# Row statistics with two homes, and 32x32 block turns by VectorE in place of TensorE's turns, in a four-layer cross-attention kernel

## The chip, the cores and the metric

The kernel runs on one core of one Trainium2 chip. The metric is the device time of one execution in microseconds (us). The core's engines run side by side, each through its own list of instructions in order, and they meet only at semaphores: TensorE (PE in the profile, PEld for its weight loads), VectorE (DVE), ScalarE (ACT), GpSimd (POOL) and SyncE (SP, which here only starts DMA transfers). Operands lie in SBUF, products of TensorE in PSUM, which has eight banks of 128 partitions by 512 numbers. All arithmetic is float32.

## What is computed

The input x and the context have 16 batches of 128 rows by 256 columns. Four layers follow each other:

```
x = L0(x, ctx)   # self attention, cross attention (16 heads of 16), then a mixture of 8 experts, 2 per row
x = L1(x, ctx)   # ten chosen rows of each batch attend to ctx and are replaced
x = L2(x, ctx, mask)
x = L3(x, ctx)   # cross attention with normed queries and a residual
```

The change is in the attention programs of L0 and L3, and in L2, which is grouped-query attention and a gated feed-forward:

```python
h, kv = rmsnorm(x, ln1), rmsnorm(ctx, ln1)
q = rope(h @ Wq)            # 16 heads of 64
k, v = rope(kv @ Wk), kv @ Wv   # 4 heads of 64, each shared by 4 query heads
p = softmax(q @ k.T / 8 + mask)  # per head 128 x 128
x = x + (p @ v) @ Wo
n = rmsnorm(x, ln2)
x = x + (silu(n @ Wgate) * (n @ Wup)) @ Wdown   # 1024 wide
```

## The kernel before

A batch has 128 rows, one to a partition. The program is a row of stages: one call of `attention` does L0's self attention and cross attention (32 batches one after the other), then routing and experts, then L1 for groups of four batches, then L2, then a second call of `attention` for L3. The whole order is written by hand: in each stage every engine has a loop over slots t, and in slot t it does parts that belong to batches t-3 to t+3.

**The attention programs (L348 on).** Slot t has the scores of batch t+1 (`scores`, L491), their maxima on VectorE (L831, two reductions of 128x1024 numbers), the maxima turned by TensorE (L630) and subtracted from the queries (L867), the scores again with keys on the partitions (`scores_turned`, L501), the exponentials on ScalarE (L737), and the products with the values (`products`, L512) of batch t-1. Normalization works in groups of GB = 4 batches. VectorE takes the statistics of batch t+11 at the end of slot t (`row_stats`, L808 to L815) into the tiles `st` and `mv`. GpSimd takes a group's `mv` when all four are there, writes the normed rows `xn_a` and, where the context is normed too (cross attention of L0), `cn_a`, with four instructions each at L769, and adds the output bias (L776). `st` and `mv` have one home for x and one for the context, each with room for one group. So `row_stats` of the first batch of group g waits until GpSimd is through with group g-1 (`hx_ok`, and `hc_ok` for the context).

**L2 (slots t = 0 to 16).** TensorE does in slot t, in this order: scores of batch t (`scores`, L2061, 32 matrix products that contract over 32 rows, four row tiles of the array at a time, into banks 0 to 3, one bank for each key head); the output projection of batch t-1 (`rows_out`, L2089); queries of t+1 (L1407 in two banks); the first of four turns of the probabilities (`turn`, L2071); keys and values of t+1 (L1420, L1423); the second turn; the turn of the middle rows of t-1 (`turn_mid`, L2096) and of the input rows of t+2 (L1432); the third turn; the gate projection `g0`, the fourth turn, `u0`, `g1`, `u1` (all L1407); the products of batch t (L2081); and the down projection of t-1 (L2089). A turn is four 128x128 transposes into bank 4, and ScalarE copies the bank to `turned_probs` (`turned_copy`, L2161). `products` makes one product of 64x512 for each key head, two of them at a time in two column halves of the array, into banks 5 and 6.

Between scores and turn a head group i goes VectorE `mask_max` (L2298, L2301), ScalarE `exps` (L2152, four instructions), VectorE `divide` (L2306), GpSimd `scale` (L2227). The middle chain of batch t-1 goes `out_copy` (L2182) on ScalarE, `rows_out` "wo", VectorE `add_rows` and `stats_mid` (L2277 to L2284), GpSimd `rms_mid` (L2221), VectorE `scale_mid` (L2290), `turn_mid`, ScalarE `mid_copy` (L2168), the gate and up projections, ScalarE `silu` (L2175), VectorE `gate` (L2312), the down projection. The table `SLOT_JOBS` says which bank each job has. `job_claim` makes TensorE wait until the bank's job before has been read out (`job_moved`).

## Time and profile before

| | us |
|---|---|
| median of 3 runs | 1411.53 |
| the runs | 1411.53, 1416.6, 1411.37 |
| the profiled execution | 1418.67 |
| its span, first to last instruction | 1416.9 |

The page of the profile gives for each engine its busy time over the span. It cannot say what an engine is worth in a stage, so the stages are read one by one: in the timelines, which list each engine's instructions with their start and with the idle time ahead of them and who ended it, and in the view of stretches, which gives the busy time of each engine and the granted clock of TensorE between two times. The attention call for L0 has its slots from about 36 to 280 us, the experts end about 700 us, L2 runs from 810 to 1246 us and L3 from 1256 us to the end.

### The profile page before, as it was taken

The page shows a single profiled execution, that of the slowest core. Times are in us where ns is not written, and L with a number is a line of the kernel's source. Part 1 is how long each engine was busy: PE and PEld are TensorE (multiplying, and loading weights), DVE is VectorE, ACT ScalarE, POOL GpSimd, SP SyncE. Part 2 cuts the span into 40 slices and gives each one's busy share as a digit, 9 for nine tenths or more (in the row PEclk, how much of TensorE's full clock was granted, in tenths as well). Part 3 has the DMA queues.
Part 4 walks back from the last instruction along what each step waited for, and adds up shares of the span by engine and source line. Part 5 has one row for each costly group of instructions (what it writes and reads, how often), then busy time and mean ns, then how long its engine had stood idle before and what let it go on. Part 6 is the DMA issues. An engine that isn't in the chain of part 4 may idle for free. (4 is left out here: it accounts for less than half of the span.)

```text
span 1416.9 us, 32778 instructions
## 1 busy us (share of the span) xinstructions
PE 1264.0 (89%) x13114; PEld 1044.7 (74%) x13114; DVE 681.5 (48%) x1613; ACT 644.4 (45%) x1496; POOL 430.3 (30%) x545
## 2 busy tenths in 40 slices
PE   4898899886799999999588799999999999858986
PEld 2566666665589999999477678888888888735665
DVE  3686777767422000000564564544544544237775
ACT  2454555422444445544212165655655655325542
POOL 3224446243323222235100152432432432123200
PEclk9999999966799999999656899999999999989997
DMA  9000000000389999997410000000000000000000
GB/s 300 2 2 2 2 2 17 9 17 23 109 299 336 330 357 355 350 341 260 156 32 2 3 1 2 1 2 1 1 1 1 2 1 2 0 0 2 17 16 31
DMA packets 80038, 120.02 MB, mean 85 GB/s; under 512 B 12112, under 2 KB 62544, under 8 KB 79760
## 3 DMA queue, kind: packets, MB, share of 16 engines
q1 hardware_dynamic: 73840, 106.62, 22.4%
q0 software_dynamic: 4768, 10.26, 2.0%
q8 instruction: 105, 1.72, 0.5%
q10 hardware_dynamic: 1280, 1.04, 0.2%
q14 instruction: 45, 0.37, 0.1%
HBM read 108.43 MB, written 9.48 MB: 83 GB/s over the span
## 5 line engine op out<-in xcount | busy, mean ns | idle before, releaser
L1590 ACT ACTIVATE w_ca<-scores,fc1b 128x128 f32<-128x128 f32 x312 | 114.2, 368 | 139.8 <-PE scores L1545 118.7
L1545 PEld LDWEIGHTS scores<-reg 128*128 128x128 f32 x1248 | 145.1, 192 | 7.8 <-DMA reg<-in_fc 2.8
L1545 PE MATMUL scores<-reg 128*128 128x128 f32 x1248 | 146.4, 275 | 4.3 <-DMA reg<-in_fc 1.8
L1555 PE MATMUL bank<-reg,w_ca 128*128 128x256 f32 x624 | 141.1, 379 | 0.3 <-DVE small L1615 0.3
L2152 ACT ACTIVATE reg<-reg,mx 128x128 f32<-128x128 f32 x256 | 99.2, 389 | 88.0 <-DVE mx L2301 87.7
L831 DVE TENSOR_REDUCE reg<-scores 128x8 f32<-128x1024 f32 x96 | 112.9, 1219 | 49.6 <-PE scores L491 49.4
L1624 DVE TENSOR_TENSOR reg<-bank,reg 128x256 f32<-128x256 f32 x39 | 16.6, 425 | 241.6 <-PE bank L1555 233.3
L2227 POOL TENSOR_TENSOR reg<-reg,rden 128x512 f32<-128x512 f32 x64 | 66.7, 1042 | 212.1 <-DVE rden L2306 212.0
L1555 PEld LDWEIGHTS bank<-reg,w_ca 128*128 128x128 f32 x624 | 115.6, 190 | 14.5 <-DVE small L1615 0.3
L1407 PE MATMUL scores<-reg 128*128 128x128 f32 x1024 | 122.0, 278 | 0.5 <-ACT reg L2168 0.5
L1407 PEld LDWEIGHTS scores<-reg 128*128 128x128 f32 x1024 | 119.3, 195 | 0.7 <-ACT reg L2168 0.7
L2089 PE MATMUL bank<-reg,w_ca 128*128 128x256 f32 x512 | 118.8, 385 | 0.8 <-issue 0.8
L2089 PEld LDWEIGHTS bank<-reg,w_ca 128*128 128x128 f32 x512 | 94.7, 190 | 26.6 <-issue 13.2
L737 ACT ACTIVATE reg<-scores 128x1024 f32<-128x1024 f32 x96 | 92.9, 1021 | 39.2 <-PE scores L501 35.7
L671 ACT ACTIVATE reg<-bank,qk_bias,shape_c 128x512 f32<-128x512 f32 x96 | 69.7, 780 | 55.5 <-PE bank L474 55.2
L501 PE MATMUL scores<-reg 32*128 32x128 f32 x1536 | 64.3, 308 | 32.6 <-DVE reg L831 31.6
L501 PEld LDWEIGHTS scores<-reg 32*128 32x128 f32 x1536 | 54.9, 208 | 48.8 <-issue 48.7
L970 POOL DMA_INDIRECT expert_out<-reg,block_ids_of x39 | 38.7, 992 | 143.7 <-DMA expert_out<-reg,block_ids_of 79.5
L2312 DVE TENSOR_TENSOR w_ca<-scores,w_ca 128x512 f32<-128x512 f32 x32 | 22.1, 692 | 109.1 <-PE scores L1407 109.1
L491 PEld LDWEIGHTS scores<-reg 32*128 32x128 f32 x1536 | 50.0, 192 | 29.8 <-ACT reg L737 21.4
L732 ACT ACTIVATE reg<-bank,shape_c 128x256 f32<-128x256 f32 x48 | 22.8, 474 | 104.3 <-DVE reg L341 104.3
L491 PE MATMUL scores<-reg 32*128 32x128 f32 x1536 | 59.7, 290 | 8.8 <-ACT reg L737 6.6
(277 smaller groups left out, 2383.7 us busy)
## 6 DMA issues: line engine op xcount, KB each, us to landing
reg<-in_fc SPq DMA_DIRECT2D x78, 1024.0 KB
reg<-expert_out SPq DMA_DIRECT2D x16, 256.0 KB, 3.7
xres<-in_x SPq DMA_DIRECT2D x4, 512.0 KB, 10.7
ctxr<-in_ctx SPq DMA_DIRECT2D x1, 2048.0 KB, 14.8
w_l<-in_w_l SPq DMA_DIRECT2D x2, 1024.0 KB, 12.1
routed_rows<-reg SPq DMA_DIRECT2D x8, 256.0 KB
out<-xres SPq DMA_DIRECT2D x8, 256.0 KB, 2.1
w_sa<-in_w_sa SPq DMA_DIRECT2D x1, 1024.0 KB, 8.6
```

Of the source, the lines that this page charges most:

```text
L491: ins = nc.tensor.matmul(S[r][:, (2 * s + c) * P:(2 * s + c + 1) * P], Qs[rows_of(r), (b // GB) % 2, s, c, batch(b)], Ks[rows_of(r), (b // ...
L501: ins = nc.tensor.matmul(S[r][:, (2 * s + c) * P:(2 * s + c + 1) * P], Ks[rows_of(r), (b // GB) % 2, s, c, batch(b)], Qs[rows_of(r), (b // ...
L671: ins = nc.scalar.activation(dst[:, g % 2, s, m, :], bank[:, :], ACT.Identity, scale=scale[:, s:s + 1], bias=bias[:, s, m:m + 1])
L737: ins = nc.scalar.activation(PT2[:, t % 2, 2 * half:2 * half + 2, :, :, :].rearrange("p r s c q -> p (r s c q)"), scores4[:, 2 * half:2 * ...
L831: ins = nc.vector.tensor_reduce(mxpad.rearrange("p (c n d) -> p n c d", c=C, d=DH)[:, 4 * half:4 * half + 4, :, 0], scores4[:, 2 * half:2 ...
L1407: ins = nc.tensor.matmul(bank[:, k * P:(k + 1) * P], w[:, c, w0:w0 + P], src[:, c, :], start=(c == 0), stop=(c == C - 1))
L1545: ins = nc.tensor.matmul(S[n % 4][:, 0:P], up_w8[j % 2][:, c, f * P:(f + 1) * P], xbT[:, j % 2, c, :], start=(c == 0), stop=(c == C - 1))
L1555: ins = nc.tensor.matmul(T[j % 2][:, 0:D], h1[:, j % 2, f, :], down_w8[j % 2][:, f, :], start=(f == 0), stop=(f == FC - 1))
L1590: nc.scalar.activation(h1[:, j % 2, f, :], S[n % 4][:, 0:P], ACT.Gelu, bias=fc1b[:, bass.ds(e * FC + f, 1)]).then_inc(M["fc1_free"], 1)
L2089: ins = nc.tensor.matmul(bank[:, 0:D], src[:, f, :], w[:, f, :], start=(f == 0), stop=(f == FC - 1))
L2152: ins = nc.scalar.activation(v[:, a, :], v[:, a, :], ACT.Exp, bias=cols_of(mx, n)[:, a:a + 1], accum_out=cols_of(psum, n)[:, a:a + 1])
L2227: nc.gpsimd.tensor_tensor(v, v, spread(rden, n), ALU.mult).then_inc(M["l2_scaled"], 1)
```

## The change

It has two parts.

**Two homes for row statistics.** `st` and `mv` get four places in place of two: a pair (x, context) for even groups and one for odd groups. `row_stats` of group g now waits for GpSimd's group g-2, and only from g = 2 on.

**L2's probabilities are turned by VectorE.** The transposes of TensorE and ScalarE's copies go. `turn` is now one VectorE instruction for each head group, SBUF to SBUF, which transposes each 32x32 block within its place: a row strip of 32 partitions then holds, for the 32 query rows of that strip, 32 keys on the partitions in each of four blocks k. So `products` contracts over 32 rows at a time: for each strip r of four, key block k of four and key head of four one product of 64x128, 64 in all, accumulated over k. Strip r has a bank of its own (0 to 3), two key heads use its column halves. Each strip needs all values at its own 32 partitions. SyncE therefore writes the values of each batch to DRAM (`values_dram`, 128 KB) and reads them back four times (4 x 128 KB) into `values4`, which lies in `w_sa`. `out_copy` is four copies of 128x256 in place of two of 128x512. The order of the slot and `SLOT_JOBS` change with it: `turn_in` and `turn_mid` come ahead of keys and values, the transposed middle rows and the down projection use bank 4, and GpSimd does `rms_mid` ahead of all four `scale`s.

The core of the diff:

```diff
-        st = sb("st", [P, 2, GB, 6])
-        mv = sb("mv", [P, 2, GB, 2])
+        st = sb("st", [P, 4, GB, 6])
+        mv = sb("mv", [P, 4, GB, 2])
...
-                        if g > 0 and j == 0:
-                            dve.wait_ge(M["hx_ok"], GB * g)
-                            if norms == 2 and stage_of(g - 1)["kv"] == "norm":
-                                dve.wait_ge(M["hc_ok"], GB * (g % G))
+                        if g > 1 and j == 0:
+                            dve.wait_ge(M["hx_ok"], GB * (g - 1))
+                            if norms == 2 and stage_of(g - 2)["kv"] == "norm":
+                                dve.wait_ge(M["hc_ok"], GB * (g % G - 1))
+                        k = 2 * (g % 2)
...
-        SLOT_JOBS = [("wo", -1, "a"), ("qa", 1, "b"), ("qb", 1, "c"), ("kv", 1, "a"), ("xt", -1, 0), ("at", 2, 1),
-                     ("g0", -1, 2), ("u0", -1, 3), ("g1", -1, 0), ("u1", -1, 1), ("pv0", 0, "a"), ("pv1", 0, "b"), ("d", -1, "c")]
+        SLOT_JOBS = [("wo", -1, "a"), ("qa", 1, "b"), ("qb", 1, "c"), ("at", 2, 0), ("xt", -1, "t"), ("kv", 1, "a"),
+                     ("g0", -1, 1), ("u0", -1, 2), ("g1", -1, 3), ("u1", -1, 0),
+                     ("pv0", 0, 0), ("pv1", 0, 1), ("pv2", 0, 2), ("pv3", 0, 3), ("d", -1, "t")]
...
+                for b in range(B):
+                    sp.wait_ge(M["l2_values_ok"], b + 1)
+                    if b >= 2:
+                        await_done(sp, "pv3", b - 2)
+                    own_rows = values_dram[b * P:(b + 1) * P, :]
+                    sp.dma_start(own_rows, values2[:, b % 2, :, :].rearrange("p h d -> p (h d)")).then_inc(values_out, 16)
+                    sp.wait_ge(values_out, 16 * (b + 1))
+                    for r in range(4):
+                        sp.dma_start(values4[32 * r:32 * r + 32, b % 2, :, :], own_rows.rearrange("(k p) n -> p k n", p=32))\
+                            .then_inc(values_in[b % 2], 16)
...
                 def products(b):
                     pe.wait_ge(M["l2_pt_ok"], 4 * b + 4)
-                    pe.wait_ge(M["l2_values_ok"], b + 1)
+                    pe.wait_ge(values_in[b % 2], 16 * 4 * (b // 2 + 1))
+                    out_banks = [job_claim(pe, f"pv{r}", b) for r in range(4)]
                     for q in range(2):
-                        bank = job_claim(pe, f"pv{q}", b)
-                        for half in range(2):
-                            i = 2 * q + half
-                            ins = nc.tensor.matmul(bank[half * HD:(half + 1) * HD, :], values2[:, b % 2, i, :],
-                                                   turned_probs[:, b % 2, A4 * i:A4 * (i + 1), :].rearrange("p a q -> p (a q)"),
-                                                   start=True, stop=True)
-                        ins.then_inc(job_done(f"pv{q}", b), 1)
+                        for k in range(4):
+                            for half in range(2):
+                                i = 2 * q + half
+                                for r in range(4):
+                                    own = slice(32 * r, 32 * r + 32)
+                                    ins = nc.tensor.matmul(out_banks[r][half * HD:(half + 1) * HD, q * P:(q + 1) * P],
+                                                           values4[own, b % 2, k, i * HD:(i + 1) * HD],
+                                                           turned_probs[own, b % 2, A4 * i:A4 * (i + 1), 32 * k:32 * k + 32],
+                                                           start=(k == 0), stop=(k == 3))
+                                    if q == 1 and k == 3 and half == 1:
+                                        ins.then_inc(job_done(f"pv{r}", b), 1)
...
+                def turn(b, i):
+                    n = 4 * b + i
+                    dve.wait_ge(M["l2_scaled"], n + 1)
+                    if b >= 2:
+                        await_done(dve, "pv3", b - 2)
+                    nc.vector.transpose(turned_tile(n).rearrange("p a k -> p (a k)"), bank_of(n)[0].rearrange("p a k -> p (a k)"))\
+                        .then_inc(M["l2_pt_ok"], 1)
```

TensorE, one steady slot of L2, before. The first row is `scores`; L2071 is a turn:

```order
L2061 MATMUL scores<-reg 128x128 x32
L2089 MATMUL bank<-reg,w_ca 128x256 x8
L1407 MATMUL bank<-reg 128x128 x16
L2071 MATMUL bank<-ident,reg 128x128 x4
L1420 MATMUL bank<-reg 128x128 x4
L1423 MATMUL bank<-reg 128x256 x2
L2071 MATMUL bank<-ident,reg 128x128 x4
L2096 MATMUL scores<-ident,reg 128x128 x2
L1432 MATMUL scores<-ident,reg 128x128 x4
L2071 MATMUL bank<-ident,reg 128x128 x4
L1407 MATMUL scores<-reg 128x128 x8
L2071 MATMUL bank<-ident,reg 128x128 x4
```

The rows go on with a turn, 24 of L1407 (`u0`, `g1`, `u1`), L2081 and L2089. The same slot in the changed kernel, L2076 being `scores`, L2100 a projection of rows, L1412 queries and then gate and up, L2090 the products:

```order
L2076 MATMUL scores<-reg 128x128 x32
L2100 MATMUL bank<-reg,w_ca 128x256 x8
L1412 MATMUL bank<-reg 128x128 x16
L1437 MATMUL scores<-ident,reg 128x128 x4
L2107 MATMUL bank<-ident,reg 128x128 x2
L1425 MATMUL bank<-reg 128x128 x4
L1428 MATMUL bank<-reg 128x256 x2
L1412 MATMUL scores<-reg 128x128 x32
L2090 MATMUL scores<-reg,w_sa 64x128 x64
L2100 MATMUL bank<-reg,w_ca 128x256 x8
L2076 MATMUL scores<-reg 128x128 x32
```

The four turns are gone from between the projections, the products stand in the same place with 64 instructions in place of 4 and write the banks named `scores`, and the next slot's scores follow after the down projection.

VectorE in a slot of L2, before, from the fourth maximum to the second multiply (L2306 `divide`, L1475 and L1476 `rope` of the queries, L2290 `scale_mid`, L2312 `gate`):

```order
L2301 TENSOR_REDUCE mx<-reg 128x4
L2306 RECIPROCAL rden<-psum 128x4
```

In the changed kernel (L2285 the fourth maximum, L2290 `divide`, L2297 the new turn, L2304 `gate`, L1461 the statistics of the inputs):

```order

```

The four turns stand between the rope products and the statistics of batch t+3. The second multiply, L2304 again, comes after these statistics, as before.

## Rows read from the trace of the kernel before

**Rows 1.** the page, part 1: busy us of TensorE, share of the span, instructions.

```profile
PE 1264.0 (89%) x13114; PEld 1044.7 (74%) x13114; DVE 681.5 (48%) x1613; ACT 644.4 (45%) x1496; POOL 430.3 (30%) x545
```

**Rows 2.** timeline of TensorE, one steady slot: start us, us, line, form, count, idle before.

```profile
854.13 2.07 PE L2061 MATMUL scores<-reg 32*128 32x128 f32 x64
856.13 3.72 PE L2089 MATMUL bank<-reg,w_ca 128*128 128x256 f32 x16
859.69 3.73 PE L1407 MATMUL bank<-reg 128*128 128x128 f32 x32
863.26 0.60 PE L2071 MATMUL bank<-ident,reg 128*128 128x128 f32 x4
863.69 1.06 PE L1420 MATMUL bank<-reg 128*128 128x128 f32 x8
...
866.92 0.63 PE L2071 MATMUL bank<-ident,reg 128*128 128x128 f32 x4 [0.21 <-ACT reg L2161]
...
869.61 5.52 PE L1407 MATMUL scores<-reg 128*128 128x128 f32 x48
875.06 1.94 PE L2081 MATMUL bank<-reg 128*64 128x512 f32 x8
876.93 3.72 PE L2089 MATMUL bank<-reg,w_ca 128*128 128x256 f32 x16
880.58 1.62 PE L2061 MATMUL scores<-reg 32*128 32x128 f32 x48
```

**Rows 3.** timeline of VectorE, same slot: the second multiply of the gated feed-forward.

```profile
875.17 0.69 DVE L2312 TENSOR_TENSOR w_ca<-scores,w_ca 128x512 f32<-128x512 f32 x1 [1.94 <-PE scores L1407]
```

**Rows 4.** timeline of TensorE, stage of chosen tokens: two forms in small tiles.

```profile
784.40 1.90 PE L1719 MATMUL scores<-reg,w_ca 32*32 32x128 f32 x128
...
794.12 3.77 PE L1737 MATMUL scores<-w_ca,reg 32*128 32x32 f32 x128
```

**Rows 5.** groups by line and form, whole span: busy us, mean ns; idle before.

```profile
L2152 ACT ACTIVATE reg<-reg,mx 128x128 f32<-128x128 f32 x256 | 99.2, 389 | 88.0 <-DVE mx L2301 87.7
...
L2227 POOL TENSOR_TENSOR reg<-reg,rden 128x512 f32<-128x512 f32 x64 | 66.7, 1042 | 212.1 <-DVE rden L2306 212.0
...
L2298 DVE SCALAR_TENSOR_TENSOR reg<-scores,reg 128x512 f32<-128x512 f32 x64 | 43.5, 679 | 19.7 <-PE scores L2061 19.7
...
L341 DVE STREAM_TRANSPOSE reg<-bank 128x512 f32<-128x512 f32 x48 | 34.1, 711 | 11.2 <-PE bank L512 9.6 <-remote 1.4
...
L2168 ACT ACTIVATE reg<-scores 128x256 f32<-128x256 f32 x16 | 6.1, 380 | 10.0 <-PE scores L2096 10.0
```

**Rows 6.** timeline of TensorE, the last slot that has products.

```profile
1218.89 1.94 PE L2081 MATMUL bank<-reg 128*64 128x512 f32 x8
```

**Rows 7.** the page, part 6: DMA issues: count, KB each, us to landing.

```profile
reg<-expert_out SPq DMA_DIRECT2D x16, 256.0 KB, 3.7
```

**Rows 8.** timeline of three engines around one stop, first attention program.

```profile
119.23 4.85 POOL L769 TENSOR_SCALAR reg<-ctxr,mv,rstd 128x256 f32<-128x256 f32 x4
...
124.17 0.43 DVE L808 BATCH_NORM_STATS2 st<-xres 128x6 f32<-128x256 f32 x1 [6.66 <-issue]
...
127.59 2.09 PE L501 MATMUL scores<-reg 32*128 32x128 f32 x32 [4.25 <-DVE reg L831]
```

**Rows 9.** the line of the row statistics: what ended its idle time, us, times.

```profile
  issue: 18.1, 3
```

**Rows 10.** busy us of engines by stretch: PE, PEld, DVE, ACT, POOL; then clock granted.

```profile
80.51:97.05 16.54, 16.48 (x229) 11.59 (x230) 13.44 (x27) 8.86 (x13) 8.46 (x9) 1.00 0.01 2
111.29:134.84 23.55, 19.30 (x229) 13.65 (x230) 13.29 (x28) 8.96 (x13) 15.06 (x16) 0.86 0.01 2
149.01:170.14 21.13, 18.46 (x233) 12.30 (x234) 13.32 (x28) 10.64 (x16) 15.11 (x16) 1.00 0.01 2
184.31:206.73 22.42, 20.07 (x233) 13.47 (x234) 13.99 (x31) 10.75 (x16) 15.07 (x16) 0.92 0.01 2
1287.61:1306.05 18.44, 16.70 (x225) 10.86 (x226) 12.64 (x23) 10.57 (x15) 7.76 (x8) 1.00 0.01 2
```

119 lines of the change are left out of this document (48 added, 71 removed).

## Prediction, made before the changed kernel was run

> **What bounds the kernel now.** I read the page first: TensorE is busy for 89% of the span [rows 1], so a change pays where it shortens TensorE's list or a wait of TensorE. Both parts sit in stages that repeat, so I went on to timelines of one slot each. In L2 the steady slot is 26.45 us long, from one `scores` to the next (854.13 to 880.58), and TensorE is without work in it for 0.21 us only, ahead of the third turn [rows 2]. VectorE meanwhile stands idle for 1.94 us even ahead of the slot's last multiply [rows 3]. So L2 is bound by TensorE's list, and work moved to VectorE is free until a chain gets late. In the attention programs the heavy slots are TensorE's too, but in the cross attention of L0 there are three stops in which VectorE waits at the row statistics, 18.1 us in all [rows 9]. The profile calls them "issue". The rows of the first one say what it is: GpSimd's four normalizations of the context start at 119.23 and take 4.85 us, and VectorE goes on at 124.17, after 6.66 us; TensorE then stood still for 4.25 us until 127.59 [rows 8].
>
> **Part 1, two homes for statistics.** The stop is a wait of group g's first statistics for GpSimd's group g-1. What is queued behind it on VectorE are the maxima of the next batch, which TensorE needs for the turned scores. With two homes the wait is for group g-2, which GpSimd ended four slots earlier, so the stop goes. What is late next is TensorE itself, which used part of the stop to work ahead; the gain is therefore not 18.1 us. I compare pairs of slots with and without a stop [rows 10]. [...] That is 7.0 us. Cross attention without one, from the last program: 18.44 us; with one 21.13 and 22.42, so 2.7 and 4.0 us. Sum 13.7 us. The last program has two such waits before its slots get going; there TensorE is not ready earlier, and I count nothing. Bounds: 8.1 us, if each stop gives back only the second one's 2.7, with no help of the clock, and 18.1 us, VectorE's whole idle time [rows 9].
>
> **Part 2, L2, a steady slot.**
> - Removed from TensorE: four turns. One takes 0.43 us of its list (863.26 to 863.69), four 1.72, and the wait of 0.21 goes with them: -1.93 us [rows 2].
> - Products: before 1.87 us (875.06 to 876.93) [rows 2]. Now 64 products, each two records as all float32 products here, so 128 records of 128 columns in tiles of 32x64, eight of them in the array. No row shows this form. With four tiles (`scores`) 64 records take 2.00 us (854.13 to 856.13) [rows 2], 31 ns each, 125 ns for each tile. With sixteen tiles of 32x32 and also 128 columns, 128 records take 1.90 us, 14.8 ns each [rows 4]. Eight tiles at 125 ns each would give 15.6 ns, above the 14.8 that the chip keeps up: 2.0 us. I take 2.0 us, +0.13. Ends: 1.9 us by sixteen tiles, 4.0 us if only four tiles run at a time.
> - A new wait. The products' four banks are 0 to 3, and bank 0 holds `u1` until VectorE's second multiply has read it. Before, that multiply ran beside the products: it starts at 875.17 and takes 0.69 [rows 3], and the products start at 875.06 [rows 2]. Now they can start at 875.86: +0.80 us. Behind the wait on TensorE stand the products and the down projection, nothing that another engine could cover.
> - The next slot's scores need the same four banks, so four copies of 128x256 on ScalarE, at most 0.38 each [rows 5] or 1.5 us. They run beside the down projection, 3.65 us [rows 2]: nothing.
> - VectorE gets four turns. The nearest row is the 32x32 turn of 128x512 out of PSUM, 0.71 us; the multiply of the same size takes 0.68 [rows 5]. 2.8 us in a slot in which VectorE has idle time to spare. Their place decides. From the slot's start: scores end at 2.0; maximum pairs take twice 0.68 us; the third pair now waits for the output projection (856.13 to 859.69, so 5.6) and the middle statistics and ends at 8.2; then the exponentials of group 2 (four of 0.39) at 9.8, those of group 3, after two copies, at 12.3; GpSimd's fourth scale (1.04) at 14.4 [rows 5]. VectorE, in its order, reaches turn 3 at about 16.1 after the first multiply and ends at 16.8. TensorE ends `u1` at 26.45 less turns and wait (1.93), products (1.87) and down projection (3.65), which is 19.0. So the turns have over 2 us of cover; a slot 2 us faster would lay them bare.
> - The middle chain: `turn_mid` now stands at about 9.6 on TensorE; the scaled middle rows are ready at about 8.7, ScalarE's copy at 10.7; gate and up projections take 4/3 of the 5.45 us that three of their four parts show (869.61 to 875.06) [rows 2], 7.3, so they start at 19.0 - 7.3 = 11.7. Covered by 1 us. GpSimd's `rms_mid` ahead of the scales puts these back by 1.4 us, within the 2 us above.
> - Values through DRAM: a write and four reads of 128 KB. A read of 256 KB lands in 3.7 us [rows 7], so some 8 us, with over 30 us between the values' copy and the products. SyncE has nothing else queued in L2. Nothing.
>
> So -1.93 + 0.13 + 0.80 = -1.00 us in a slot, and there are 14 such slots (t = 1 to 14): -14.0.
>
> **The slots at the ends.** t = 15 has no queries and keys. Slot starts lie 26.45 us apart, so it starts at 880.58 + 12 x 26.45 = 1198.0, and its products at 1218.89 [rows 6], 20.9 in. There turns and gate projection wait for each other. Now the gate projections can start with the middle copy at 10.6 and end at 17.9, the products start at 18.7: -2.2, with their own +0.13 it is -2.1. t = 0 has no down projection: the next scores wait openly for the last copies, some 1.3 us, the chain of turns behind rope products on VectorE costs about 0.5 and the products 0.13: +1.9. L2 together: -14.0 - 2.1 + 1.9 = -14.2 us.
>
> **Sum.** 13.7 + 14.2 = 27.9 us. Against the profiled execution, 1418.67, this gives 1390.8. That execution is 7.1 us over the median of the runs; the same saving from the median 1411.53 gives 1383.6; I forecast 1383.5.
>
> [...] The row of the sixteen tiles has a record every 14.8 ns [rows 4]. [...]
>
> **The rivals.**
> 1. *The width of the weights counts.* With weights 128 wide and only 32 columns to stream, 128 records take 3.77 us, 29.5 ns each; with weights 32 wide 14.8 [rows 4]. A straight line between gives 19.7 ns for 64, or 2.5 us. 16 slots by 0.5 us: 1391.5. Against it: with 125 ns for a tile, a load half as wide as in `scores` should hide.
> 2. *A charge for each record binds.* Halfway between the same two rows lie 22 ns, 2.8 us: 16 slots by 0.8: 1396.5. Against it: the 14.8 ns are themselves a bound on any such charge. [...]
> 3. *Four tiles at a time.* If column halves of a row strip exclude each other, 4.0 us: +2.0 in 16 slots, 32 us, against 27.9 saved: 1415.5. Against it: the old products already ran two column halves at once (their 128*64 form), and the sixteen tiles beat this rate by two.
> 4. *Slower: load and stream of a row strip follow each other.* A record of 128 columns takes 3.57 us / 32 = 112 ns (859.69 to 863.26) on the whole array [rows 2], a load of 64 columns half of 4 x 29.5, so 59 ns. Together 171 ns, over four strips 43 ns a record and 5.5 us: +3.5 in 16 slots is 56 us, 1439.5. Slower begins where the products pass 3.8 us, 29 ns a record. Against it: sixteen tiles of 32x32 spend 4 x 14.8 = 59 ns a record and strip, less than the 112 of the stream alone. [...]
> 5. *Part 1 gives less.* Each stop gives 2.7 us, 8.1 in all, and the clock does not change: 1389.
>
> **Chances.** Forecast 0.58, rival 5 0.08, rival 1 0.12, rival 2 0.10, rival 3 0.07, rival 4 0.05. The range 1375 to 1406 leaves out rivals 3 and 4 and a little on both sides: the forecast with all 18.1 us of part 1 and products of 1.9 us is 1377.5, rival 2 with 8.1 us of part 1 is 1402, and about 3 us either way are the spread of the runs (1411.37 to 1416.6). About 0.5%, 7 us, is what a measurement of this kernel can tell from no change. Below 1404.5: 0.82; within 7 us of 1411.5: 0.11; above: 0.07.
>
> **What would show it.** Right: the L2 slot at about 25.45 us; the products' 128 records in 2.0 us; 0.8 us idle ahead of them, ended by the second multiply; no idle time of VectorE at the row statistics from 110 to 200 us, the pairs of slots at 16.5 and 18.4. Wrong: products above 2.5 us, TensorE waiting for the new VectorE turn, or for the middle copy ahead of the gate projection; a half clock where TensorE was warm.

## The result and the profile after

The changed kernel takes 1392.85 us (median of 4 runs, 1389.38 to 1398.77), the kernel before 1412.88 us in the runs beside it (4 runs, 1411.37 to 1416.6): ratio 0.9859, 95% interval 0.9819 to 0.9899, or 20.0 us less. The forecast was 1383.5 in a range of 1375 to 1406. The time is inside the range and on the side that was forecast, 9.3 us above the point; most of what follows is about these 9 us. The profiled execution of the changed kernel took 1392.40 us, span 1390.6; that of before 1418.67, span 1416.9.

The page, part 1 (busy us of each engine, share of the span, instructions), to be read beside [rows 1]. TensorE lost 34 us of work and is busy for 88% of the span; VectorE's busy time grew by 48 us, and its turns alone take 43.6:

```profile
PE 1230.0 (88%) x14778; PEld 1035.2 (74%) x14778; DVE 729.9 (52%) x1677; ACT 611.3 (44%) x1464; POOL 428.7 (31%) x545
```

The groups by line, new or changed (busy us, mean ns of one, then the idle time ahead of them and what ended it):

```profile
L2297 DVE STREAM_TRANSPOSE reg<-reg 128x512 f32<-128x512 f32 x64 | 43.6, 689 | 0.0
...
L2090 PE MATMUL scores<-reg,w_sa 32*64 32x128 f32 x2048 | 35.0, 282 | 19.2 <-issue 14.2 <-DVE reg L2297 5.1
...
L2176 ACT ACTIVATE w_ca<-scores 128x256 f32<-128x256 f32 x64 | 19.4, 390 | 69.5 <-PE scores L2090 69.5
...
L2274 DVE TENSOR_SCALAR reg<-xres,small 128x256 f32<-128x256 f32 x16 | 17.2, 1073 | 2.2 <-POOL small L2208 1.5
```

A turn on VectorE takes 689 ns (forecast from rows of 0.68 and 0.71 us) and VectorE never waited ahead of one. One copy of the products takes 390 ns (380). The products' idle time of 14.2 us is put down to "issue", and 5.1 to the turns, which is the first slot alone. The last row is a surprise: VectorE's scale of the middle rows took 1073 ns on average, where the same instruction took 0.34 us in most slots before.

**A steady slot of L2.** TensorE's timeline (start us, us, line, form, count, idle time before), the slot that answers to [rows 2]:

```profile
862.95 2.07 PE L2076 MATMUL scores<-reg 32*128 32x128 f32 x64
864.94 3.72 PE L2100 MATMUL bank<-reg,w_ca 128*128 128x256 f32 x16
868.50 3.73 PE L1412 MATMUL bank<-reg 128*128 128x128 f32 x32
872.07 0.60 PE L1437 MATMUL scores<-ident,reg 128*128 128x128 f32 x4
872.51 0.40 PE L2107 MATMUL bank<-ident,reg 128*128 128x128 f32 x2
...
874.50 7.31 PE L1412 MATMUL scores<-reg 128*128 128x128 f32 x64
882.75 2.09 PE L2090 MATMUL scores<-reg,w_sa 32*64 32x128 f32 x128 [0.94 <-issue]
884.76 3.96 PE L2100 MATMUL bank<-reg,w_ca 128*128 128x256 f32 x16
888.65 0.61 PE L2076 MATMUL scores<-reg 32*128 32x128 f32 x12
```

From 862.95 to 888.65 it is 25.70 us; this one has a down projection of 3.96 us, most have 3.72 and last 25.46 to 25.48. The mean of the fourteen is 25.50 us, where before had 26.45. The 128 records of the products (L2090; a record is one row of the trace, and each of the 64 products leaves two) run from 882.75 to the next start at 884.76: 2.01 us, 15.7 ns each. They start after 0.94 us without work. VectorE in the same slot:

```profile
871.29 1.12 DVE L2274 TENSOR_SCALAR reg<-xres,small 128x256 f32<-128x256 f32 x1
...
876.10 0.70 DVE L2297 STREAM_TRANSPOSE reg<-reg 128x512 f32<-128x512 f32 x1
...
876.78 0.68 DVE L2297 STREAM_TRANSPOSE reg<-reg 128x512 f32<-128x512 f32 x1
...
878.02 0.69 DVE L2297 STREAM_TRANSPOSE reg<-reg 128x512 f32<-128x512 f32 x1
878.64 0.65 DVE L2304 TENSOR_TENSOR w_ca<-scores,w_ca 128x512 f32<-128x512 f32 x1
879.21 0.69 DVE L2297 STREAM_TRANSPOSE reg<-reg 128x512 f32<-128x512 f32 x1
...
881.85 0.69 DVE L2304 TENSOR_TENSOR w_ca<-scores,w_ca 128x512 f32<-128x512 f32 x1 [1.02 <-PE scores L1412]
```

From the fourth maximum on VectorE's order is: the rope products of the queries, the first two turns with a reciprocal between them, the rope products of the keys, the third turn, the first multiply of the feed-forward, the fourth turn, the statistics of batch t+3, the second multiply. The four turns end at 879.9, 2.9 us ahead of the products. The slot's second multiply (L2304, the last row) starts when `u1` is done, and ends at 882.54; the products start 0.2 us behind that. So the wait stands where the forecast put it, although the profile names it "issue".

**Part 1.** The stops at the row statistics (L811, L808 before) are gone: no "issue" as in [rows 9] is left in the line's idle time, which lists 5.3 us for the first load of x and 10.3 us for TensorE at the start of L3. Windows over pairs of slots, from score to score (busy us of PE, PEld, DVE, ACT, POOL with their counts, then the granted clock), answering to [rows 10]:

```profile
110.73:127.27 16.54, 16.49 (x229) 11.60 (x229) 14.40 (x32) 9.19 (x13) 14.90 (x16) 1.00 0.01 3
141.43:159.88 18.45, 18.40 (x232) 12.28 (x233) 15.04 (x32) 11.15 (x16) 15.29 (x16) 1.00 0.01 2
174.04:192.49 18.45, 18.40 (x232) 12.28 (x233) 15.45 (x30) 11.15 (x16) 15.11 (x16) 1.00 0.01 1
```

16.54 us in self attention and 18.45 in cross attention, which are the 16.54 and 18.44 of the pairs without a stop; all at the full clock (1.00).

**The slots at the ends.** The first slot (t = 0) and the last with products (t = 15):

```profile
791.29 3.79 PE L2076 MATMUL scores<-reg 32*128 32x128 f32 x64 [1.78 <-DVE xres L2023]
...
806.92 3.65 PE L2090 MATMUL scores<-reg,w_sa 32*64 32x128 f32 x128 [5.07 <-DVE reg L2297]
812.00 2.07 PE L2076 MATMUL scores<-reg 32*128 32x128 f32 x64 [1.43 <-ACT w_ca L2176]
```

```profile
1169.03 2.07 PE L2076 MATMUL scores<-reg 32*128 32x128 f32 x64
...
1178.55 0.44 PE L2107 MATMUL bank<-ident,reg 128*128 128x128 f32 x2 [3.81 <-DVE reg L2274]
1179.46 8.81 PE L1412 MATMUL scores<-reg 128*128 128x128 f32 x64 [0.47 <-ACT reg L2162]
1189.21 2.09 PE L2090 MATMUL scores<-reg,w_sa 32*64 32x128 f32 x128 [0.94 <-issue]
```

The first slot takes 20.71 us, and took 17.65 before (810.04 to 827.69 in that trace). The last one takes 20.18 from its scores to its products; before it was 20.95. Its gate and up projections took 8.81 us, since the granted clock was 0.50 of full speed from 1179.0 to 1182.4; 7.31 us is what they take in the steady slot above, at 1.00.

**Where the 26.3 us between the two spans went.** Up to the first product of the routing: 262.76 before, 249.57 after, -13.2. From there to the first scores of L2, where the change touches nothing: 547.3 and 541.7, -5.6. First slot +3.1, fourteen steady slots -13.2, t = 15 to the start of L3 -0.6, L3 +3.2.

### The profile page after: what moved, and what is told of

It reads as the page before. It is cut to its first block and busy times, and to the rows that moved or that the text cites. A ratio compares the mean times of both kernels' runs of the same rounds, so it can differ in the third digit from the quotient of the medians.

```text
span 1390.6 us, 36276 instructions
## 1 busy us (share of the span) xinstructions
PE 1230.0 (88%) x14778; PEld 1035.2 (74%) x14778; DVE 729.9 (52%) x1677; ACT 611.3 (44%) x1464; POOL 428.7 (31%) x545
## 3 DMA queue, kind: packets, MB, share of 16 engines
q8 instruction: 118, 1.93, 0.6%
q10 hardware_dynamic: 1280, 1.04, 0.2%
## 5 line engine op out<-in xcount | busy, mean ns | idle before, releaser
L1560 PEld LDWEIGHTS bank<-reg,w_ca 128*128 128x128 f32 x624 | 115.6, 190 | 14.4 <-DVE small L1620 0.3
L1412 PEld LDWEIGHTS scores<-reg 128*128 128x128 f32 x1024 | 119.7, 196 | 2.1 <-ACT reg L2162 1.4
L1412 PE MATMUL scores<-reg 128*128 128x128 f32 x1024 | 120.2, 279 | 0.9 <-ACT reg L2162 0.9
L2100 PE MATMUL bank<-reg,w_ca 128*128 128x256 f32 x512 | 119.0, 386 | 0.9 <-issue 0.8
L2100 PEld LDWEIGHTS bank<-reg,w_ca 128*128 128x128 f32 x512 | 94.7, 190 | 17.4 <-issue 4.0
L503 PE MATMUL scores<-reg 32*128 32x128 f32 x1536 | 60.7, 297 | 23.3 <-DVE reg L834 23.3
L503 PEld LDWEIGHTS scores<-reg 32*128 32x128 f32 x1536 | 51.5, 199 | 38.8 <-issue 38.7
L2261 DVE TENSOR_TENSOR xres<-bank,xres 128x256 f32<-128x256 f32 x32 | 13.6, 424 | 110.4 <-PE bank L2100 110.4
L493 PEld LDWEIGHTS scores<-reg 32*128 32x128 f32 x1536 | 49.8, 194 | 28.3 <-ACT reg L739 21.3
L2205 POOL TENSOR_TENSOR small<-small 128x1 f32<-128x1 f32 x16 | 3.1, 193 | 205.0 <-DVE small L2268 205.0
L493 PE MATMUL scores<-reg 32*128 32x128 f32 x1536 | 59.0, 292 | 7.9 <-ACT reg L739 7.3
```

What stands on the lines that cost most here:

```text
L493: ins = nc.tensor.matmul(S[r][:, (2 * s + c) * P:(2 * s + c + 1) * P], Qs[rows_of(r), (b // GB) % 2, s, c, batch(b)], Ks[rows_of(r), (b // ...
L503: ins = nc.tensor.matmul(S[r][:, (2 * s + c) * P:(2 * s + c + 1) * P], Ks[rows_of(r), (b // GB) % 2, s, c, batch(b)], Qs[rows_of(r), (b // ...
L1412: ins = nc.tensor.matmul(bank[:, k * P:(k + 1) * P], w[:, c, w0:w0 + P], src[:, c, :], start=(c == 0), stop=(c == C - 1))
L1560: ins = nc.tensor.matmul(T[j % 2][:, 0:D], h1[:, j % 2, f, :], down_w8[j % 2][:, f, :], start=(f == 0), stop=(f == FC - 1))
L2100: ins = nc.tensor.matmul(bank[:, 0:D], src[:, f, :], w[:, f, :], start=(f == 0), stop=(f == FC - 1))
```

## Experiments

All are of the same kernel family; ratios are to the kernel before in the runs beside them, which gave 1413.87 us (17 runs) for the first four, 1418.28 (7 runs) for the next four and 1420.33 (8 runs) for the last three. The kernels of the last two groups are therefore compared by their ratios and by their traces.

**1 and 2. Each part alone.** First the kernel before with the two homes and nothing else:

```diff
-        st = sb("st", [P, 2, GB, 6])
+        st = sb("st", [P, 4, GB, 6])
...
-                        if g > 0 and j == 0:
-                            dve.wait_ge(M["hx_ok"], GB * g)
+                        if g > 1 and j == 0:
+                            dve.wait_ge(M["hx_ok"], GB * (g - 1))
...
```

> The kernel before with part 1 alone: st and mv have two homes, row_stats waits for GpSimd's group g-2. My theory: the three stops of VectorE in the cross attention of L0 go (7.0 + 2.7 + 4.0 us by pairs of slots), so 13.7 us less than before, and the start of L3 stays as it is. Rival A, part 1 is worth its stops and nothing else but moves TensorE's clock windows at the start of L3 for the worse, as the changed kernel's trace shows there (slots of 8.5, 10.0 and 10.1 us in place of 6.9, 9.2 and 9.3): then 10 to 11 us less and the same long slots in this kernel's L3. Rival B, the fall of the clock there is chance: the L3 slots are short here.

Measured: 1401.27 us (6 runs), ratio 0.9914, interval 0.9897 to 0.9931, or 12.6 us less. The first product of the routing stands at 249.04, 13.7 us before that of the kernel before. That this is the term of part 1 to the tenth is partly luck, since the point varies by more than 1 us between executions: it stands at 261.40 and not at 262.76 in the next kernel, which has one home too, and at 248.2 to 250.1 in the other traces with two. At least a part of that comes from the clock long before the stops: the granted clock was 0.50 for 3.4 us from about 55 us on in the traces of the kernel before, the changed one and this one, and 1.00 there in those of experiments 2 and 3. Traces that are alike in this give 13.2 and 13.7 us for part 1, and 12.4 (261.40 against 248.98).

L3 took 161.7 us here from its first product to the end, against 157.9 in the kernel before, as rival A expects. But in the traces of experiments 4 and 6, which have two homes too, it took 157.4 and 157.9, and in that of experiment 2, with one home, 161.1. So the homes don't decide it; rival B, chance, is what is left.

Then the changed kernel with the same lines put back, that is, the turns on VectorE alone:

> The changed kernel with part 1 undone: one home for the statistics, all of L2 as changed. My theory: the stops in L0 are back (13 to 14 us over the changed kernel), L2's slot is 25.5 us and its products take 2.0 us as in the changed kernel. From scores of batch 0 to the first product of L3 the changed kernel needs 10.8 us less than the kernel before; so this one should be 10 to 11 us faster than before. Rival: with part 1 gone the L3 start is fast again, then 13 to 14 us.

Measured: 1405.76 us (6 runs), ratio 0.994, interval 0.9919 to 0.996, or 8.1 us less; expected were 10 to 11. In its trace L2 takes 10.1 us less than before from its first scores to the start of L3, and L3 3.2 us more. The two parts add up to 20.7 us, and the change as a whole measured 20.0: no sign that they work on each other. The whole is short of 27.9 mainly by the second part (8.1 against 14.2), less by the first (12.6 against 13.7). In this kernel, too, nothing is changed from the routing to L2, and the stretch took 543.6 us; in the kernel with the homes alone it took 540.8. In the kernels of experiments 5, 6, 7 and 11, which have the same work there as the changed one, it took 546.7 to 547.2. So it varies by several us between executions, and the -5.6 above are not shown to be the change's.

**3. The wait for bank 0.** The second up-projection goes to a bank that is free at that time:

```diff
-                      ("g0", -1, 1), ("u0", -1, 2), ("g1", -1, 3), ("u1", -1, 0),
+                      ("g0", -1, 1), ("u0", -1, 2), ("g1", -1, 3), ("u1", -1, "b"),
```

> The changed kernel with one entry of SLOT_JOBS changed: u1 goes to bank 6 (home b, free since the rope of the queries) in place of bank 0. My theory: the wait of 0.94 us ahead of the products is that for u1's bank, so it goes, VectorE's second multiply runs beside the products again, and nothing else is near: slot 25.50 - 0.94 = 24.56 us, 14 slots and t = 15, 14 us less than the changed kernel. Rival: another wait stands right behind it (the fourth VectorE turn, or the values from DRAM), then 0 to 5 us and the profile names it.

Measured: 1377.14 us (5 runs, 1375.05 to 1380.37), ratio 0.9744, interval 0.9726 to 0.9762: 15.7 us faster than the changed kernel, and faster than both. TensorE's timeline has no idle time at the products:

```profile
879.12 1.95 PE L1412 MATMUL bank<-reg 128*128 128x128 f32 x16
881.00 2.10 PE L2090 MATMUL scores<-reg,w_sa 32*64 32x128 f32 x128
```

Slots are 24.48 us apart, 1.02 less than in the changed kernel. That shows what the 0.94 us of "issue" were: the wait for the reader of bank 0, with its semaphore.

**4. How many tiles run at a time.** The changed kernel with the column half as the outermost loop of the products, so that four tiles are in use at a time and not eight:

```diff
-                    for q in range(2):
-                        for k in range(4):
-                            for half in range(2):
+                    for half in range(2):
+                        for q in range(2):
+                            for k in range(4):
```

> The changed kernel with the loops of products in another order: all of column half 0 first, then all of half 1, so that only the four row strips of one half can run at the same time; same 64 products. Theory 1, a tile gives one record of 128 columns in 125 ns and the number of tiles at work decides: 128 records at 31 ns, 4.0 us in place of 2.0, +2.0 in 16 slots, 32 us slower than the changed kernel. Theory 2, a charge of some 15 to 16 ns for each record decides and tiles don't: still 2.0 us, no change.

Measured: 1409.64 us (10 runs), ratio 0.9978, interval 0.996 to 0.9996: 16.8 us slower than the changed kernel, halfway between the two theories. The products:

```profile
889.92 3.36 PE L2090 MATMUL scores<-reg,w_sa 32*64 32x128 f32 x128 [0.94 <-issue]
893.22 3.72 PE L2100 MATMUL bank<-reg,w_ca 128*128 128x256 f32 x16
```

128 records in 3.30 us are 25.8 ns each, 103 ns for each of four tiles. Tiles count, so the forecast's account stands only in part: eight tiles are needed for 2.0 us, but a tile of 32x64 comes free after 103 ns and not after the 125 of `scores` with its 128 columns of weights. By 103 ns eight tiles would give 12.9 ns a record; what they do give is 15.7. So something other than the tiles sets the products' pace in the changed kernel.

**5. The fourth turn ahead of the input statistics.** This part of the change undone:

```diff
-                    if now:
-                        turn(t, 3)
                     if is_batch(t + 3):
                         l2_stats_in(dve, link, t + 3)
+                    if now:
+                        turn(t, 3)
```

> The change with its smallest part undone: the fourth turn stands behind the input statistics on VectorE again. In the trace of the change the fourth turn ends 16.9 us into a slot, the statistics behind it take 1.2 us (four instructions, 0.38 + 0.41 + 0.18 + 0.15), and the products start at 19.8. Theory 1: the move is worth nothing, since the turn would end at 18.1 and still be 1.7 us early: the slots stay at 25.50 us and the total at 1393 us, within 2. Rival: the products' idle time of 0.94 us is in truth a wait for the fourth turn (the profile infers releasers): then the slots grow by up to 1.2 us, to 26.7, and the total by up to 19 us, to 1412.

Measured: 1400.52 us (4 runs), ratio 0.9863, interval 0.9825 to 0.99; the change has 0.9859. Most slots are 25.46 to 25.50 us apart, with the same 0.94 us ahead of the products. This move is worth nothing, and the wait isn't one for the turn.

**6. The length of the cover.** In the kernel of experiment 3 the fourth turn goes behind the second multiply, to the very end of VectorE's slot:

```diff
-                    if now:
-                        turn(t, 3)
...
                     if before_now:
                         gate(t - 1, 1)
+                    if now:
+                        turn(t, 3)
```

> The change with the second up-projection in a bank of its own (1377.1 us), and with the fourth turn as VectorE's last work of a slot, behind the second gating multiply. In that kernel's trace this multiply ends at 881.80, 0.80 us after the products start (881.00), so the fourth turn would end at 882.5. Theory 1: the wait is now in sight and costs what the times say: the products start 1.5 us later, and with some 0.15 us for the semaphore a slot takes 24.48 + 1.6 = 26.1 us; over 16 slots some 25 us, 1402. It tells how long the cover of the turns is: 1.9 us in that kernel, from the turn's end at 879.1 to the products at 881.0. Rival: the products' start isn't set by the turns even then (TensorE would be late for another reason): 1377.

Measured: 1401.12 us (4 runs), ratio 0.9883, interval 0.985 to 0.9916, against 0.9744. The products now wait for the turn:

```profile
862.04 2.09 PE L2090 MATMUL scores<-reg,w_sa 32*64 32x128 f32 x128 [1.40 <-DVE reg L2297]
```

The slots grow from 24.48 to 25.95 us, by 1.47 (expected 1.6). So the cover of the turns (the time for which a late turn costs nothing) ends where the times say, and the releaser that the profile names is here the right one.

**7. The scale that takes three times as long.** In the kernel of experiment 3 GpSimd's first multiply waits until VectorE has scaled the middle rows:

```diff
                         for i in range(4):
+                            if i == 0 and is_batch(t - 1):
+                                pool.wait_ge(M["l2_mid_ok"], t)
                             scale(t, i)
```

> The change with the second up-projection in a bank of its own, and GpSimd's first scaling of a slot waits until VectorE has scaled the middle rows. Theory 1: the middle scale took 1.12 us in place of 0.35 because GpSimd's 1.04 us multiply ran beside it; now it takes 0.35 us again, at the same start (8.3 us into the slot), and GpSimd's scaling starts 0.4 us later, which its cover hides. The steady slot stays at 24.48 us; in the last slot (t=15), where TensorE waits for the middle rows, 0.8 us are won. Total 1376.3, not to be told from 1377.1 by the time alone; the row of the scale decides. Rival: the longer scale comes from something else (its place behind the reciprocal, its operand): it stays at 1.1 us.

Measured: 1378.86 us (4 runs), ratio 0.9712, interval 0.9682 to 0.9742. In the changed kernel VectorE's scale starts at 871.29 (above), and GpSimd's timeline has, for its first two multiplies:

```profile
871.22 2.08 POOL L2214 TENSOR_TENSOR reg<-reg,rden 128x512 f32<-128x512 f32 x2
```

With the wait VectorE's scale reads:

```profile
873.85 0.35 DVE L2276 TENSOR_SCALAR reg<-xres,small 128x256 f32<-128x256 f32 x1
```

and GpSimd's multiplies behind it:

```profile
874.28 2.04 POOL L2214 TENSOR_TENSOR reg<-reg,rden 128x512 f32<-128x512 f32 x2 [0.47 <-DVE reg L2276]
```

1.12 us beside GpSimd's multiply, 0.35 without it. In the kernel before the scale took 0.34 us, because GpSimd's order was another: its third multiply started at 863.58 and took 1.04, and VectorE's scale came as that ended:

```profile
864.60 0.34 DVE L2290 TENSOR_SCALAR reg<-xres,small 128x256 f32<-128x256 f32 x1
```

That trace confirms the cause by itself. In its slot t = 15 GpSimd's third multiply started at 1207.38, just ahead of the scale, and the scale was the only long one of its 16:

```profile
1207.41 1.16 DVE L2290 TENSOR_SCALAR reg<-xres,small 128x256 f32<-128x256 f32 x1
```

In both traces the scale ends with the multiply that it met: in the changed kernel it started 0.07 us after a multiply of 1.04 us (871.22) and ended 0.15 us after that multiply, and in the kernel before, at t = 15, it started 0.03 us after one of 1.04 us and ended 0.15 us after it. The 32x32 turns kept their 0.7 us beside the same multiplies: the second, at 876.78, took 0.68 with GpSimd's fourth multiply from 876.94 on. Why the scale is held up and the turn is not, no row shows. In the slot t = 15 TensorE waits 3.04 us for the middle rows, where it was 3.81, and the 0.77 us are what the scale lost. They don't reach the end: there three of the four projections behind it took 8.07 us in place of the 7.47 of experiment 3, at a mean granted clock of 0.68 in place of 0.74, and from scores to products the slot took 20.0 against 19.9. In the steady slots, too, the long scale is covered: they are 24.45 us apart with the wait and 24.48 without. The total can't tell the two kernels apart.

**8. Column halves that follow each other.** In the kernel of experiment 3, eight tiles as before, but the two halves of a row strip directly one behind the other:

```diff
-                            for half in range(2):
-                                i = 2 * q + half
-                                for r in range(4):
-                                    own = slice(32 * r, 32 * r + 32)
+                            for r in range(4):
+                                own = slice(32 * r, 32 * r + 32)
+                                for half in range(2):
+                                    i = 2 * q + half
```

> The change with the second up-projection in a bank of its own, and in the products the two column halves of one row strip follow each other (the four row strips outside), in place of four row strips of one column half and then four of the other. Eight tiles are in use in both. Theory 1: what counts is how many records pass before a tile comes again (8 in both), so 128 records take 2.0 us as before and the total stays at 1377. Rival: two records in a row on one row strip hold each other up, as two loads of weights into the same rows would: then a pair costs up to what a row strip's record costs in the scores (31 ns), 64 pairs 2.0 to 4.0 us, up to 2.0 us more in each of 16 slots, up to 1409.

Measured: 1380.34 us (4 runs), ratio 0.9742, interval 0.9706 to 0.9778, as experiment 3. 128 records again take 2.02 us, in slots of 24.48. This order within the eight tiles made no difference, and a row strip took two records in a row at no price: rivals 3 and 4 of the prediction don't hold even there.

**9 and 10. What sets 15.7 ns.** In the kernel of experiment 3 each record is split into two of 64 columns; the products are the same, the weights are loaded twice as often:

```diff
-                        for k in range(4):
+                        for c, k in [(c, k) for c in range(2) for k in range(4)]:
                             for half in range(2):
...
-                                    ins = nc.tensor.matmul(out_banks[r][half * HD:(half + 1) * HD, q * P:(q + 1) * P],
+                                    ins = nc.tensor.matmul(out_banks[r][half * HD:(half + 1) * HD, at:at + 64],
...
-                                                           turned_probs[own, b % 2, A4 * i:A4 * (i + 1), 32 * k:32 * k + 32],
+                                                           turned_probs[own, b % 2, a0:a0 + 2, 32 * k:32 * k + 32],
```

> The change with the second up-projection in a bank of its own (slot 24.48 us, 1377.1 us), with each instruction of the products split into two of 64 columns: 256 records in place of 128 for the same products, eight tiles in turn as before, the same weights loaded twice. Theory 1: with eight tiles a record costs a charge of its own of about 15.7 ns, whatever its columns: the products take 4.0 us in place of 2.0, a slot 26.5 us, the total 1377 + 16 x 2.0 = 1409. Rival: the columns that stream through the tiles set the time (103 ns for 128 columns in one tile, shared by eight, is 12.9 ns): 64 columns cost half, the products stay at 2.0 to 2.1 us and the total at 1377.

And the same with the column half outermost, four tiles at a time:

> The kernel with the split columns, and the column half as the outermost loop, so that only four tiles are in use at a time: 256 records of 64 columns. With 128 records of 128 columns over four tiles a record took 25.8 ns, 103 ns for a tile. Theory 1: most of a tile's 103 ns is the load of its weights and the streaming of 128 columns, one behind the other; with 64 columns the tile takes 103 less the time of 64 columns, by their pace at full clock in the keys' products of this kernel (32 records of 128 columns in 1.95 to 3.73 us, 58 to 61 ns each on a single tile) some 29 ns: 74 ns a tile, 18.5 ns a record, 4.7 us for 256 records, so a slot of 27.2 us. Rival: the tile is kept by its columns alone (0.8 ns a column): 51 ns a tile, 12.9 ns a record, which the charge of a record lifts to 15.7: 4.0 us, as with eight tiles, and a slot of 26.5 us.

Measured: 1432.66 us (5 runs), ratio 1.0084, interval 1.0052 to 1.0116, and one run of 1430.92. TensorE at the products, eight tiles first:

```profile
892.11 1.65 PE L2091 MATMUL scores<-reg,w_sa 32*64 32x64 f32 x134
895.07 1.54 PE L2091 MATMUL scores<-reg,w_sa 32*64 32x64 f32 x122 [1.32 <-issue]
...
947.43 2.46 PE L2091 MATMUL scores<-reg,w_sa 32*64 32x64 f32 x207
951.82 0.78 PE L2091 MATMUL scores<-reg,w_sa 32*64 32x64 f32 x49 [1.93 <-issue]
```

and four tiles:

```profile
892.48 2.10 PE L2091 MATMUL scores<-reg,w_sa 32*64 32x64 f32 x134
...
948.29 3.15 PE L2091 MATMUL scores<-reg,w_sa 32*64 32x64 f32 x207
```

134 records take 1.65 us and 207 take 2.46, so 0.81 / 73 = 11.1 ns for each with eight tiles, and (3.15 - 2.10) / 73 = 14.4 ns with four. In four tiles, then, a record holds its tile for 58 ns with 64 columns and for 103 with 128: there the columns count, 0.7 ns each (an estimate from these two figures), beside some 12 ns of something else. In eight tiles half the columns bring 15.7 down to 11.1 ns only, though the tiles would allow 58 / 8 = 7.2. So neither theory holds as written: a record isn't charged 15.7 ns whatever its columns, and the tiles' own time isn't what limits eight of them. What does stays open. The 74 ns for a tile in the expectation of the four tiles rest on a row read wrongly: 1.95 us is the time of 16 such records and 3.73 that of 32, so one takes 112 to 122 ns and not 58 to 61.

The whole time is worse still, for a reason that none of them expected: TensorE stands idle once inside the products of every slot but the first, for 1.3 to 2.2 us with eight tiles and 0.7 to 1.6 with four, put down to "issue". It comes after 134, 170 and 207 of the 256 records in three successive slots, so it isn't tied to a step of the kernel. And in every slot it comes after the same number of records in both kernels, within one (189, 225, 134, 170, 207, 243, 152 in the first seven that have it), although the paces differ: the place in TensorE's list decides, and not the time. In the first slot, where the 256 records took 3.96 us at a mean granted clock of 0.58 (eight tiles), there is no stop. No semaphore is waited for inside this loop; what TensorE waits for there is not shown.

**11. The first slot.** In the kernel of experiment 3, and at t = 0 alone, VectorE does the turns ahead of the rotary products:

```diff
+                    if t == 0:
+                        for i in range(4):
+                            if i >= 2:
+                                divide(t, i)
+                            turn(t, i)
                     if after_now:
                         l2_rope_queries(dve, t + 1, 0)
...
```

> The change with the second up-projection in a bank of its own, and in the first slot alone VectorE does the four turns ahead of the rotary products of the second batch, which stand before and between them elsewhere. In that kernel's first slot TensorE waits 4.93 us for the fourth turn, which ends at 808.35. Theory 1: the turns then follow GpSimd's scaling: ScalarE's last exponential ends at 804.94, so the fourth turn ends about 807.1 and the products start 1.2 us earlier; but the rotary products end 0.5 us later and GpSimd's sums with them, so that the scores of the second batch start 0.5 to 1.2 us earlier: a first slot of 19.3 to 20.0 us in place of 20.48, the total 1376.3, not to be told from 1377.1; the first slot's rows decide. Rival: the rotary sums take the place of the wait: the first slot stays at 20.5 us or grows by up to 1 us.

Measured: 1385.67 us (4 runs), ratio 0.9755, interval 0.9731 to 0.9779, against 0.9744: no gain. The rival was right:

```profile
795.83 3.80 PE L2076 MATMUL scores<-reg 32*128 32x128 f32 x64 [1.78 <-DVE xres L2023]
...
810.96 3.14 PE L2090 MATMUL scores<-reg,w_sa 32*64 32x128 f32 x128 [4.43 <-DVE reg L2297]
816.79 3.79 PE L2076 MATMUL scores<-reg 32*128 32x128 f32 x64 [2.69 <-POOL reg L2240]
```

The products wait 0.5 us less (4.43 in place of 4.93), but the second batch's scores now wait 2.69 us for GpSimd's rotary sums and run at a granted clock of 0.50. The slot is 20.96 us, against 20.48. The larger price stands one slot later: since the granted clock was 0.50 from 811.8 to 822.2, for all of those scores and the first 1.7 us of the output projection (3.79 and 4.46 us in place of 2.07 and 3.72), the second slot took 26.94 us, against 24.47.

## Why the prediction was right, and what it missed

**Part 1, -13.7 us: right.** -13.2 in the profiled execution, -13.7 in the trace with the homes alone and -12.6 by its medians, and the pairs of slots came out as 16.54 and 18.45 us. Measuring the pairs and not VectorE's idle time (18.1 us) was the decisive choice; rival 5 (8.1 us) is out, since the interval of experiment 1 begins at 9.8 us. To the tenth it is luck: traces give 12.4 to 13.7 (experiment 1). The 7.0 us of the first stop are the difference of the first two pairs in [rows 10]; no run shows them as a cost of the stop alone, since the longer pair had a granted clock of 0.50 for 6.8 us (126.7 to 133.5), and in the changed kernel the pair there took 16.54 us at 1.00.

**The steady slot, -1.00 us: right, with two small errors that cancel.** What stands ahead of the products, without the wait, became 2.06 us shorter in place of 1.93 (from 20.93 to 18.87 us). The products took 2.01 us against 2.0. The new wait is 0.94 us in place of 0.80; the step counted the multiply's 0.69 us and 0.11 ahead of it, and left out the 0.21 us from the multiply's end (882.54) to the products' start. Fourteen slots gave -13.2 against -14.0, part of it a few longer down projections. But the reason given for 2.0 us was wrong in its number, so that the right time came by luck: a tile comes free after 103 ns and not 125 (experiment 4), and eight tiles are held to 15.7 ns by something else (experiments 9 and 10). Rivals 1, 2, 3 and 4 are out as prices: 2.5, 2.8, 4.0 and 5.5 us didn't come. Of rival 2's idea, a charge for each record, something is left: in eight tiles it can be no more than the 11.1 ns of a record of 64 columns, half of the 22 that the rival gave it.

**The turns' cover: right.** The fourth turn was done 16.9 us into the slot, forecast 16.8, and without the wait the products start 18.8 us into the slot, forecast 19.0 (experiment 3); experiment 6 finds the end of the cover. The values' way through DRAM was hidden, too: the page, part 6, has (count, KB each, us to landing)

```profile
w_sa<-grouped_values SPq DMA_DIRECT2D x64, 128.0 KB, 2.6
...
grouped_values<-reg SPq DMA_DIRECT2D x16, 128.0 KB, 1.7
```

**t = 15, -2.1 us: mis-sized, -0.6.** The products started 20.2 us into the slot, not 18.7. The step that failed is the end of the gate projections, "start with the middle copy at 10.6 and end at 17.9": they did start at 10.4, but took 8.81 us instead of 7.3, since the granted clock had fallen to 0.50 for 3.4 of them, after TensorE had stood without work for 3.81 us. The scaled middle rows were ready at 9.5 and not at 8.7, because the scale took 1.12 us and not 0.35; the copy behind them was quick enough to make up for it. Neither is new in this slot. In the kernel before, too, the scale of t = 15 took 1.16 us (experiment 7), and the granted clock was 0.50 from 1208.7 to 1212.1. The step took its times from the steady slot, though the trace before had the slot itself. In the steady slots it is the change that made the scale long, by moving GpSimd's statistics ahead of its multiplies, and there it is covered.

**t = 0, +1.9 us: mis-sized, +3.1.** The open copies were sized right (the scores wait 1.43 us, forecast 1.3). What the step left out is the clock: TensorE had nothing to do for 5.07 us ahead of the products, and then they took 3.65 us instead of 2.0, with the granted clock at 0.50 from 806.8 to 810.2. Before, three waits of 0.7 to 1.2 us with turns between them stood there. It is not shown that the long wait alone is to blame. In the kernel with the homes alone, where L2 is the old one with its three waits, the granted clock fell in the same place (0.50 from 805.5 to 808.9), and the old products took 3.52 us instead of 1.94:

```profile
805.62 3.52 PE L2082 MATMUL bank<-reg 128*64 128x512 f32 x8 [0.69 <-ACT reg L2162]
```

That first slot took 19.23 us, 1.6 more than the 17.65 of the same L2 in the kernel before. With the turns on VectorE the clock had fallen there in every trace (means of 0.50 to 0.68 over the products), with the old turns in one of two; so up to 1.6 of the 3.1 us may be no more than the execution to which the change is compared.

**Not in the sum: L3, +3.2 us.** Its program is the same, but in the changed kernel's profiled execution the granted clock fell to 0.50 in two of its slots (1254.1 to 1257.5 and 1267.8 to 1271.2), and in the kernel before in none. In the kernel of experiment 5, whose steady slots are the same, it fell in one, in that of experiment 6 in none, and with the homes alone, whose L2 is the old one, in one. From its first product to the end L3 took 157.9 us before, 161.2 in the changed kernel, 161.7 with the homes alone, 161.4 in experiment 5 and 157.9 in experiment 6. So it varies without L2's change, and is a part of the 3 us either way that the range allowed.

**The base.** The sum was made against an execution of 1418.67 us and its saving taken off the median. That execution was slower than all 17 of the same kernel beside experiments 1 to 4 (1408.75 to 1417.84), though in the middle of the 15 beside the later ones (1414.05 to 1423.16), and its stretch from the routing to L2 was 3.5 to 6.5 us longer than in the kernels of experiments 1 to 3, which have the same work there. That stretch alone is 5.6 of the 6.3 us by which the spans differ more (26.3) than the medians (20.0); taking the saving off the median was right. If the terms of the profiled execution are put on the median, the 7.9 us between 27.9 and 20.0 are 0.5 (part 1), 0.8 (steady slots), 1.5 (t = 15), 1.2 (t = 0) and 3.2 (L3), together 7.2. How much of L3's share the median really holds isn't settled, since only one execution was profiled.

## What to carry to other kernels

When work leaves the engine that sets the pace, look first at which buffer the shortened list now reaches too early. Here one shared bank held back 15.7 us, almost as much as the whole change brought, and another bank for one projection gave 1377.1 us. Count the price of an idle stretch of TensorE together with the work behind it: in the first slot what came after 5 us without work took 3.65 us, at a mean granted clock of 0.53, instead of 2.0. Read a slot at the end of a stage from its own rows, not from the steady slot: for t = 15 they had shown both the long scale (1.16 us) and the granted clock of 0.50. And before a difference between two traces is put down to a change, look at the same stretch in a third. Where a rate is read from another tile shape, vary the number of tiles and the columns before building on the reason; the right number came here from a wrong one.

## What the runs showed that was not expected

- Records with small tiles at a granted clock of 1.00: of 128 columns in tiles of 32x64 take 15.7 ns with eight tiles in turn and 25.8 ns with four; of 64 columns 11.1 and 14.4 ns.
- A VectorE scale of 128x256 by one value per row takes 0.35 us alone and 1.12 us when a GpSimd multiply of 1.04 us has just begun. The 32x32 turns of 128x512 (0.69 us) and the rotary products (0.68), which also ran beside GpSimd's multiplies, and the first gating multiply (0.65), beside a rotary sum of GpSimd (1.27), kept their times.
- With 256 such records in a row in place of 128, TensorE stood idle once inside the loop in every slot but the first, for 0.7 to 2.2 us, after the same number of records whether eight or four tiles were in use.
- Stretches with the same work differ between executions: 541 to 547 us from the routing to L2, 157.4 to 161.7 us for L3, and 17.65 and 19.23 us for the first slot of the old L2.
- What the profile calls "issue" had three meanings in this case: VectorE's wait for GpSimd two slots of work away [rows 8, 9], TensorE's wait for the reader of a bank (0.94 us, experiment 3), and a stop inside a loop without any wait (experiments 9 and 10).
